# First filter layer over 64 rows, issued between the filter and the node sums; on ScalarE and VectorE the message ahead of the softplus

## The chip, the cores and the metric

The kernel runs on one core of a Trainium2 chip. Its time is the device time of one execution in microseconds (us). The five engines of the core run their own instruction streams side by side and meet at semaphores: TensorE (PE; its weight loads are listed as PEld), VectorE (DVE), ScalarE (ACT), GpSimd (POOL), and SyncE (SP), which here only issues transfers.

## The reference

One layer of a continuous-filter graph network over 6250 nodes and 200000 edges, sorted by `dst`:

```
h    = relu(layernorm(x))
y    = h @ W_in                                        # 6250 x 128
W_ij = (softplus(f_ij @ W_f1 + b_f1) - ln 2) @ W_f2 + b_f2   # per edge, f_ij has 20 values
m    = y[dst] * (W_ij * cutoff)                        # per edge
out  = segment_sum(m, src)                             # random scatter over the nodes
x    = x + (softplus(out @ W_o1 + b_o1) - ln 2) @ W_o2 + b_o2
```

## The kernel before

**Chunks and steps.** The edges are cut into 391 chunks of 512 (four tiles of 128). The main loop is written out as a sequence of steps k = -2, -1, 0, ...; in each step every engine does its part of several chunks, in an order fixed by the code (`hybrid_steps` calls each engine's `step`). Every engine executes its list strictly in that order and waits at semaphores.

**Two ways to sum.** Of every 25 chunks, 7 go "on PE" (108 in all): their messages are sorted into bins by matmuls with a 0/1 matrix (`bin_up`, L1289, seven tiles of four matmuls for each chunk), evacuated by ACT (`take_binned`, L729), and added to the nodes by further matmuls (`add_nodes`, L1308, twelve matmuls that alternate between rows 0 to 63 and 64 to 127 of the array). The other 283 chunks are "pool chunks": their rows with equal target are summed within a tile by `same_product` (L1275), evacuated by ACT (`take_sums`, L719 and L720), and added to memory by four indirect transfers that POOL issues (`scatter`, L598).

**The edge network of a chunk n.** `hidden_product` (L1258) is the first layer: two fp32 products of 256 edges each; the one takes rows 0 to 19 of `attrT` and `w_f1`, the other rows 64 to 83, so that they stand in two row groups of the array. Its results lie in PSUM banks 4 and 5. ACT does `softplus` in three dependent passes (L711 abs, L713 exp, L715 ln), DVE joins them with the product in `combine` (L1011), which raises `hidden_ready` (`s_h`). `filter_product` (L1266 for the bias, L1268 for the second layer) reads that. Beside it, PE fetches y[dst] by a product with a one-hot matrix (L1340, from `xwin`), ACT scales it by the cutoff (`xg`, L753), and DVE multiplies filter and xg to the message (L1099 for a pool chunk, L1096 for one on PE).

**Order in step k before.** PE: `same_product` of chunk k-2 (only if that is a pool chunk; its last quarter also waits for `hidden_ready` of chunk k, because it shares PSUM bank 5 with the first layer's result), an early `bin_up`, first layer of chunk k+1, one-hot product and filter of chunk k, one `add_nodes`, a late `bin_up`. ACT: `take_sums` of k-2, early `take_binned`, softplus of k+1, xg of k, late `take_binned`. DVE: one-hot of k+1 (L1036), node sums added (L1046), targets of k-2 (L1002, L1006), two node matrices (L1061), equality matrix of k (L995), places and payload of PE chunks (L1028, L1075, L1076, L1081), combine of k+1, message of k. There is one PSUM bank for binned tiles, so a `bin_up` waits until ACT has taken the one before (`binned_ready`).

Of the kernel before, what the change touches and what calls it, by code (L numbers as in the profile page):

```python
# [7 lines left out]
P = 128  # L8
T = 4
CE = P * T  # L10
# [12 lines left out]
def gnn_kernel(nc, x, src, src_cols, dst, dst_cols, attr_cols, cutoff_cols, W_in, W_f1, b_f1, W_f2, b_f2, W_o1, b_o1, W_o2, b_o2, out):  # L23
# [3 lines left out]
    N, F = x.shape  # L27
# [25 lines left out]
    with ctx:  # L53
        def sb(name, shape, dt=fp32):
            return ctx.enter_context(nc.sbuf_tensor(name, shape, dt))

        def sem(name):
            return ctx.enter_context(nc.semaphore(name))
# [11 lines left out]
        counting = sb("counting", [P, BINS * CAP], fp16)  # L70
        spare_row = sb("spare_row", [P, 1])
        w_in = sb("w_in", [P, F])
        w_f1 = sb("w_f1", [64 + RBF, F])
        w_f2 = sb("w_f2", [P, F])
        w_o1 = sb("w_o1", [P, F])
        w_o2 = sb("w_o2", [P, F])
# [82 lines left out]
        place_col = sb("place_col", [P, NPE, T])  # L159
        rank_max = sb("rank_max", [P, 1])  # L160

        attrT = sb("attrT", [64 + RBF, 4, CE // 2])
        dst_b = sb("dst_b", [P, 4, CE], bf16)
        src_b = sb("src_b", [P, 4, CE], i16)
        xwin = sb("xwin", [P, 4, F], bf16)
# [16 lines left out]
        s_cut = sem("cutoff_columns_loaded")  # L182
        s_iota = sem("iota_done")
        s_const = sem("constants_ready")
        s_zero = sem("zeros_ready")
        s_accz = sem("accumulators_cleared")
        s_centred = sem("centred_ready")
# [100 lines left out]
        def halves(columns):  # L288

            return columns.rearrange("p (r c) -> p r c", r=2)  # L290
# [12 lines left out]
        def exists(c):  # L303
            return 0 <= c < NCH
# [18 lines left out]
        def after(eng, semaphore, c):  # L323

            wait(eng, semaphore, c + 1)
# [69 lines left out]
        def hybrid_steps(step):  # L395

            for c in range(-2, LAST_STEP + 1):
                step(c)
# [37 lines left out]
        def _(sp):  # L436
# [58 lines left out]
            def reload_nodes():  # L495
                sp.dma_start(xs[:, :, :], x.rearrange("(p b) f -> p b f", b=NB)).then_inc(s_last, 16)

            for c in range(2):
                load_attr(c, c)
            sp.wait_ge(s_rows, 16 * 2 * G)  # L500
# [157 lines left out]
        def _(act):  # L658
# [4 lines left out]
            act.dma_start(bf1[:, :], b_f1.rearrange("(p o) -> p o", o=1)).then_inc(s_w, 16)  # L663
            for tile, a in ((bf2_row, b_f2), (bo2_row, b_o2)):
                act.dma_start(tile[:, :], a.rearrange("(o f) -> o f", o=1).to_broadcast([P, F])).then_inc(s_w, 16)
            for r in range(2):
                act.dma_start(w_f1[64 * r:64 * r + RBF, :], W_f1).then_inc(s_w, 16)

# [40 lines left out]
            def softplus(z, bias, a, steps, value):  # L709

                nc.scalar.activation(a, z, ACT.Abs, bias=bias).then_inc(steps[0], 1)  # L711
                act.wait_ge(steps[0], value)
                nc.scalar.activation(a, a, ACT.Exp, scale=-1.0).then_inc(steps[1], 1)  # L713
                act.wait_ge(steps[1], value)
                nc.scalar.activation(a, a, ACT.Ln, bias=1.0).then_inc(steps[2], 1)  # L715
# [15 lines left out]
            def hybrid_evacuations():  # L731
                def step(k):
                    n = k - 2
                    if pool_chunk(n):
                        wait(act, s_sp, pool_until(n))
                        after_scatters(act, pool_until(n - 4))
                        wait(act, s_moved, pool_until(n - 4))
                        take_sums(n % 4)
                    jobs = sorts_at.get(k, ())
                    for kk, h, i, late in jobs:  # L740
                        if not late:
                            take_binned(kk, h, i)
                    n = k + 1
                    if exists(n) and n > 0:
                        after(act, s_hp, n)
                        after(act, s_h, n - 2)
                        softplus(hidden_ps, bf1[:, 0:1], halves(hidden_exp[:, n % 2, :]), (s_size, s_exp, s_log), n + 1)
                    n = k
                    if exists(n):
                        after(act, s_xgp, n)  # L750
                        after(act, s_msg, n - 2)
                        for t in range(T):
                            last = nc.scalar.activation(xg[:, n % 2, t * F:(t + 1) * F], ps[3][:, t * F:(t + 1) * F], ACT.Copy,  # L753
                                                        scale=cut_col[:, bass.ds(n, 1), t])
                        last.then_inc(s_xg, 1)
                    for kk, h, i, late in jobs:
                        if late:
                            take_binned(kk, h, i)
                hybrid_steps(step)
# [47 lines left out]
        def _(dve):  # L807
# [8 lines left out]
            V = nc.vector  # L816
            V.memset(ones[:, :], 1.0)
            V.memset(ones_bf[:, :], 1.0)
            dve.wait_ge(s_iota, 3)
            V.tensor_scalar(ident[:, :], column_no[:, :], row_no[:, 0:1], None, ALU.is_equal)  # L820
            link(V.tensor_scalar(weight_bits[:, :], row_no[:, 0:1], -1.0, 127.0 + 63.0, ALU.mult, ALU.add))
# [187 lines left out]
            def combine(odd):  # L1009

                V.scalar_tensor_tensor(halves(hidden[:, odd, :]), hidden_ps, bf1_negative[:, 0:1], halves(hidden_exp[:, odd, :]),  # L1011
                                       ALU.max, ALU.add).then_inc(s_h, 1)

            def hybrid_work():
# [16 lines left out]
                def step(k):  # L1031
# [46 lines left out]
                    if on_pe(n):  # L1078
                        kk = pe_index[n]
                        wait(dve, s_mid, kk + 1)  # L1080
                        V.tensor_tensor(part_of(kk, 2), part_of(kk, 1), high_of(kk, 1), ALU.subtract).then_inc(s_pay, 1)  # L1081
                    n = k + 1
                    if exists(n) and n > 0:
                        after(dve, s_log, n)
                        after(dve, s_fp, n - 2)
                        combine(n % 2)
                    n = k
                    if exists(n):
                        after(dve, s_fp, n)
                        after(dve, s_xg, n)  # L1090
                        filtered = ps[2].rearrange("p (t f) -> p t f", t=T)
                        gate = xg[:, n % 2, :].rearrange("p (t f) -> p t f", t=T)
                        if on_pe(n):
                            kk = pe_index[n]
                            wait(dve, s_binps, (kk - 1) * JT)
                            V.tensor_tensor(payload[:, kk % 2, :, 0:F], filtered, gate, ALU.mult).then_inc(s_msg, 1)  # L1096
                        else:
                            wait(dve, s_sp, pool_until(n - 2))
                            V.tensor_tensor(message[:, n % 2, :, 0:F], filtered, gate, ALU.mult).then_inc(s_msg, 1)  # L1099
                hybrid_steps(step)  # L1100
                dve.wait_ge(s_accT, sums_until(NPE + SLOTS - 2, 1))

# [89 lines left out]
        def _(pe):  # L1192
# [61 lines left out]
            def hidden_product(slot):  # L1254

                for r in range(2):
                    rows = slice(64 * r, 64 * r + RBF)
                    ins = MM(hidden_ps[:, r, :], w_f1[rows, :], attrT[rows, slot, :], start=True, stop=True)  # L1258
                ins.then_inc(s_hp, 1)

# [52 lines left out]
            def hybrid_products():  # L1313
                def step(k):
                    n = k - 2
                    if pool_chunk(n):
                        wait(pe, s_same, pool_until(n))
                        after(pe, s_msg, n)
                        wait(pe, s_s, pool_until(n) - 1)
                        same_product(n % 2, range(T - 1))  # L1320
                        if exists(n + 2):
                            after(pe, s_h, n + 2)
                        same_product(n % 2, (T - 1,)).then_inc(s_sp, 1)
                    jobs = sorts_at.get(k, ())
                    for kk, h, i, late in jobs:
                        if not late:
                            bin_up(kk, h, i)
                    n = k + 1
                    if exists(n) and n > 0:
                        after_slot(pe, s_attr, n, 2)  # L1330
                        after(pe, s_h, n - 1)
                        wait(pe, s_last_sum, pool_until(n - 3))
                        hidden_product(n % 4)
                    n = k
                    if exists(n):
                        after(pe, s_oh, n)
                        after_slot(pe, s_xwin, n)
                        after(pe, s_xg, n - 1)
                        for t in range(T):
                            ins = MM(ps[3][:, t * F:(t + 1) * F], onehot[0:KW, n % 2, t * P:(t + 1) * P],  # L1340
                                     xwin[0:KW, n % 4, :], start=True, stop=True)
                        ins.then_inc(s_xgp, 1)
                        after(pe, s_h, n)
                        after(pe, s_msg, n - 1)
                        filter_product(n % 2)
                    for job in sums_at.get(k, ()):
                        add_nodes(*job)
                    for kk, h, i, late in jobs:
                        if late:
                            bin_up(kk, h, i)  # L1350
                hybrid_steps(step)
# [102 lines left out]
```

## Time and profile before

| | |
|---|---|
| median of 3 runs | 2415.03 us (2414.46 to 2416.0) |
| the profiled execution | 2413.26 us, of which the span is 2411.4 us |
| PE busy | 2207.1 us, 92% of the span |
| DVE busy | 1898.1 us, 79% |
| ACT busy | 1775.7 us, 74% |
| POOL busy | 1855.0 us, 77% |
| mean granted TensorE clock | 0.981 of full speed |

The page's section 1 gives busy shares, section 4 the chain of work that ended last (PE 71% of it), section 5 the costliest groups of instructions. A matmul's duration runs from its start to its modelled end and overlaps its neighbours; how much of PE's time a group takes is therefore read from the chain in order of time, where each piece begins at the end of the one before. Under 100 us at the start (layer norm, x W_in, sorting ranks) and some 90 us at the end (output layer) lie outside the main loop.

### The profile page before, as it was taken

The page shows a single profiled execution, that of the slowest core. Times are in us where ns is not written, and L with a number is a line of the kernel's source. Part 1 is how long each engine was busy: PE and PEld are TensorE (multiplying, and loading weights), DVE is VectorE, ACT ScalarE, POOL GpSimd, SP SyncE. Part 2 cuts the span into 40 slices and gives each one's busy share as a digit, 9 for nine tenths or more (in the row PEclk, how much of TensorE's full clock was granted, in tenths as well). Part 3 has the DMA queues.
Part 4 walks back from the last instruction along what each step waited for, and adds up shares of the span by engine and source line. Part 5 has one row for each costly group of instructions (what it writes and reads, how often), then busy time and mean ns, then how long its engine had stood idle before and what let it go on. Part 6 is the DMA issues. An engine that isn't in the chain of part 4 may idle for free.

```text
span 2411.4 us, 56737 instructions
## 1 busy us (share of the span) xinstructions
PE 2207.1 (92%) x16842; PEld 1401.0 (58%) x16842; DVE 1898.1 (79%) x3929; ACT 1775.7 (74%) x4145; POOL 1855.0 (77%) x1192
## 2 busy tenths in 40 slices
PE   1689999999999999999999999999999999999945
PEld 1566566566656656665665666566566656656623
DVE  8677877877787787878778777877887887788758
ACT  1578777777777777777777777777777777777713
POOL 2288888888887888788788888878887887888853
PEclk9899999999999999999999999999999999999968
DMA  9265556555555555555555555555555555555565
GB/s 354 100 99 91 88 88 90 87 88 88 90 87 87 90 89 88 88 90 87 87 89 87 89 89 90 86 87 91 86 89 88 89 86 88 90 87 88 81 162 180
DMA packets 351511, 239.84 MB, mean 99 GB/s; under 512 B 89459, under 2 KB 338497, under 8 KB 351071
## 3 DMA queue, kind: packets, MB, share of 16 engines
q0 software_dynamic: 164000, 77.47, 33.4%
q1 hardware_dynamic: 185987, 158.25, 24.1%
q8 instruction: 140, 2.29, 0.4%
q14 instruction: 172, 1.41, 0.2%
q10 hardware_dynamic: 1212, 0.42, 0.1%
HBM read 139.86 MB, written 96.12 MB: 98 GB/s over the span
## 4 chain that ended last, share of the span: by engine, by line
PE 71%; DMA 8%; issue 7%; DVE 5%; POOL 4%; ACT 4%; ACTq 0%; SPq 0%; POOLq 0%; DVEq 0%
PE ps L1289 20%; PE ps L1308 16%; PE ps L1268 11%; PE ps L1258 8%; PE ps L1275 8%; DMA acc<-region,target 7%; PE ps L1340 4%; POOL acc L598 4%; PE ps L1266 3%; ACT region L729 1%; ACT region L753 1%; ACT region L711 1%; ACT region L713 1%; DMA w_f<-in_L_gnn_W_f_dram 1%; DMA region<-in_x_dram 0%
## 5 line engine op out<-in xcount | busy, mean ns | idle before, releaser
L598 POOL DMA_INDIRECT acc<-region,target x1132 | 1797.1, 1588 | 424.5 <-issue 274.9
L1289 PE MATMUL ps<-region 128*128 128x386 bf16 x3024 | 650.0, 336 | 66.5 <-ACT region L729 46.6
L729 ACT ACTIVATE region<-ps 128x386 bf16<-128x386 f32 x756 | 372.3, 492 | 272.5 <-PE ps L1289 217.2
L1308 PE MATMUL ps<-region 64*128 64x448 bf16 x4536 | 497.8, 352 | 9.5 <-DVE region L1046 9.5
L1289 PEld LDWEIGHTS ps<-region 128*128 128x128 bf16 x3024 | 253.4, 97 | 367.6 <-issue 169.8
L1011 DVE SCALAR_TENSOR_TENSOR region<-ps,bf_negative,region 128x512 f32<-128x512 f32 x391 | 292.1, 747 | 210.3 <-ACT region L715 119.2
L753 ACT ACTIVATE region<-ps,cut_col 128x128 f32<-128x128 f32 x1564 | 439.0, 362 | 0.7 <-PE ps L1340 0.7
L1268 PEld LDWEIGHTS ps<-w_f,region 128*128 128x128 f32 x3128 | 414.7, 193 | 11.2
L1268 PE MATMUL ps<-w_f,region 128*128 128x128 f32 x3128 | 415.4, 276 | 0.0
L711 ACT ACTIVATE region<-ps,bf 128x512 f32<-128x512 f32 x391 | 268.6, 687 | 71.2 <-PE ps L1258 11.5
L1275 PEld LDWEIGHTS ps<-region 128*128 128x128 f32 x2264 | 294.0, 191 | 26.2 <-DVE region L1011 4.0
L1308 PEld LDWEIGHTS ps<-region 64*128 64x128 bf16 x4536 | 190.9, 94 | 197.2 <-issue 14.7
L1275 PE MATMUL ps<-region 128*128 128x129 f32 x2264 | 302.4, 275 | 2.4 <-DVE region L1011 1.3
L1061 DVE TENSOR_SCALAR region<-counting,region 128x448 bf16<-128x448 f16 x756 | 291.3, 425 | 9.0 <-PE ps L1308 8.3
L1258 PE MATMUL ps<-attrT,w_f 20*128 20x256 f32 x1564 | 276.1, 429 | 16.0 <-ACT region L719 7.3
L713 ACT ACTIVATE region<-region 128x512 f32<-128x512 f32 x391 | 246.4, 630 | 12.3
L715 ACT ACTIVATE region<-region 128x512 f32<-128x512 f32 x391 | 246.2, 630 | 12.4
L1099 DVE TENSOR_TENSOR region<-ps,region 128x512 f32<-128x512 f32 x283 | 194.8, 688 | 72.5 <-ACT region L753 38.8
L1002 DVE TENSOR_SCALAR moved<-region,weight_limit,spare_row 128x4 f32<-128x4 f32 x283 | 108.1, 382 | 126.5 <-ACT region L720 104.5
L1046 DVE TENSOR_TENSOR region<-region,ps 128x896 f32<-128x896 f32 x188 | 202.2, 1075 | 4.3 <-PE ps L1308 4.3
L1258 PEld LDWEIGHTS ps<-attrT,w_f 20*128 20x128 f32 x1564 | 118.3, 184 | 144.4 <-issue 144.4
L995 DVE TENSOR_TENSOR region<-src_b,src_col 128x512 f32<-128x512 int16 x283 | 195.6, 691 | 0.0
(128 smaller groups left out, 1700.0 us busy)
## 6 DMA issues: line engine op xcount, KB each, us to landing
dst_b<-dst_rows SPq DMA_DIRECT2D x391, 128.0 KB
src_b<-src_rows SPq DMA_DIRECT2D x283, 128.0 KB
acc<-region,target POOLq DMA_INDIRECT x1132
attrT<-in_edge_attr_dram SPq DMA_DIRECT2D x782, 20.0 KB
acc<-region SPq DMA_DIRECT2D x20, 640.0 KB, 17.4
xwin<-xw_parts SPq DMA_DIRECT2D x391, 31.5 KB
region<-acc SPq DMA_DIRECT2D x48, 256.0 KB, 4.5
xw_parts<-parts SPq DMA_DIRECT2D x12, 384.0 KB, 2.3
```

The costliest lines, as they stand in the source:

```text
L598: nc.gpsimd.indirect_dma_start(out=acc[a], out_offset=bass.IndirectOffsetOnAxis(ap=target[:, slot, t:t + 1], axis=0), in_=summed[:, slot, ...
L711: nc.scalar.activation(a, z, ACT.Abs, bias=bias).then_inc(steps[0], 1)
L713: nc.scalar.activation(a, a, ACT.Exp, scale=-1.0).then_inc(steps[1], 1)
L729: nc.scalar.activation(binned[:, h, j, :], binned_ps[:, 0:PC], ACT.Copy).then_inc(s_binned, 1)
L753: last = nc.scalar.activation(xg[:, n % 2, t * F:(t + 1) * F], ps[3][:, t * F:(t + 1) * F], ACT.Copy, scale=cut_col[:, bass.ds(n, 1), t])
L1011: V.scalar_tensor_tensor(halves(hidden[:, odd, :]), hidden_ps, bf1_negative[:, 0:1], halves(hidden_exp[:, odd, :]), ALU.max, ALU.add).then ...
L1061: V.tensor_scalar(in_node[:, sums_until(kk, i) % 2, slot, :], counting[:, 0:NL], binned[:, slot, j, 3 * F:3 * F + 1], binned[:, slot, j, 3 ...
L1258: ins = MM(hidden_ps[:, r, :], w_f1[rows, :], attrT[rows, slot, :], start=True, stop=True)
L1268: ins = MM(ps[2][:, t * F:(t + 1) * F], hidden[:, odd, t * P:(t + 1) * P], w_f2[:, :], start=False, stop=(t == T - 1), skip_group_check=True)
L1275: ins = MM(sums_ps[t], same[:, odd, t * P:(t + 1) * P], message[:, odd, t, :], start=True, stop=True)
L1289: ins = MM(binned_ps[:, 0:PC], place[:, h % 2, t, j * P:(j + 1) * P], payload_high[:, h % 2, t, :], start=(t == 0), stop=(t == T - 1))
L1308: ins = MM(ps[6 + r][:, 0:NL], binned[rows, slot, j, part * F:(part + 1) * F], in_node[rows, sums_until(kk, i) % 2, slot, :], start=(d == ...
```

## The change

The first layer now works on 64 rows in each half: `w_f1` and `attrT` are allocated with 128 rows, cleared by DVE at the very start, and only 20 rows of each half are loaded as before; the others stay zero. SP and ACT wait for the clearing before they load into them. In the main loop the first layer of chunk k+1 is issued after the filter of chunk k and directly ahead of `add_nodes`; on ACT xg of chunk k stands ahead of the softplus of k+1; on DVE the message of chunk k stands ahead of the combine of k+1. `general_*`, the path for other inputs, is not run here and keeps its order.

```diff
-        w_f1 = sb("w_f1", [64 + RBF, F])
+        w_f1 = sb("w_f1", [P, F])
-        attrT = sb("attrT", [64 + RBF, 4, CE // 2])
+        attrT = sb("attrT", [P, 4, CE // 2])
+            sp.wait_ge(s_blank, 2)
             for c in range(2):
                 load_attr(c, c)
+            act.wait_ge(s_blank, 1)
             for r in range(2):
                 act.dma_start(w_f1[64 * r:64 * r + RBF, :], W_f1).then_inc(s_w, 16)
...
             V.memset(ones_bf[:, :], 1.0)
+            V.memset(w_f1[:, :], 0.0).then_inc(s_blank, 1)
+            V.memset(attrT[:, :, :], 0.0).then_inc(s_blank, 1)
...
-                    rows = slice(64 * r, 64 * r + RBF)
+                    rows = slice(64 * r, 64 * r + 64)
                     ins = MM(hidden_ps[:, r, :], w_f1[rows, :], attrT[rows, slot, :], start=True, stop=True)
...
# PE, step k (ACT: softplus behind xg; DVE: combine behind the message, in the same manner)
-                    n = k + 1
-                    if exists(n) and n > 0:
-                        after_slot(pe, s_attr, n, 2)
-                        after(pe, s_h, n - 1)
-                        wait(pe, s_last_sum, pool_until(n - 3))
-                        hidden_product(n % 4)
                     n = k
                     if exists(n):
                         after(pe, s_oh, n)
...
                         filter_product(n % 2)
+                    n = k + 1
+                    if exists(n) and n > 0:
+                        after_slot(pe, s_attr, n, 2)
+                        after(pe, s_h, n - 1)
+                        wait(pe, s_last_sum, pool_until(n - 3))
+                        hidden_product(n % 4)
                     for job in sums_at.get(k, ()):
                         add_nodes(*job)
```

PE's list in the middle of the main loop, before: one step from `same_product` (L1275) to `add_nodes` (L1308). A bracket holds the semaphores an instruction waits for.

```order
L1275 MATMUL ps<-region 128x129 [waits sums_ready,message_ready,same_ready]
L1275 MATMUL ps<-region 128x129 x2
L1275 MATMUL ps<-region 128x129 [waits hidden_ready]
L1289 MATMUL ps<-region 128x386 [waits binned_ready]
L1289 MATMUL ps<-region 128x386 x3
L1258 MATMUL ps<-attrT,w_f 128x256 [waits last_sums_ready,hidden_ready,attr_loaded1]
L1258 MATMUL ps<-attrT,w_f 128x256
L1340 MATMUL ps<-xwin,onehot 128x128 [waits xg_ready,window_loaded0,onehot_ready]
L1340 MATMUL ps<-xwin,onehot 128x128 x3
L1266 MATMUL ps<-bf_parts,ones_bf 128x512 [waits message_ready,hidden_ready]
L1268 MATMUL ps<-w_f,region 128x128 x4
L1308 MATMUL ps<-region 128x448 [waits node_sums_added,in_node_ready]
```

The same step of the changed kernel, where the lines are 1280 for `same_product`, 1294 for `bin_up`, 1339 for the one-hot product, 1271 and 1273 for the filter, 1263 for the first layer and 1313 for `add_nodes`:

```order
L1280 MATMUL ps<-region 128x129 [waits sums_ready,message_ready,same_ready]
L1280 MATMUL ps<-region 128x129 x2
L1280 MATMUL ps<-region 128x129 [waits hidden_ready]
L1294 MATMUL ps<-region 128x386 [waits binned_ready]
L1294 MATMUL ps<-region 128x386 x3
L1339 MATMUL ps<-xwin,onehot 128x128 [waits xg_ready,window_loaded0,onehot_ready]
L1339 MATMUL ps<-xwin,onehot 128x128 x3
L1271 MATMUL ps<-bf_parts,ones_bf 128x512 [waits message_ready,hidden_ready]
L1273 MATMUL ps<-w_f,region 128x128 x4
L1263 MATMUL ps<-attrT,w_f 128x256 [waits last_sums_ready,hidden_ready,attr_loaded1]
L1263 MATMUL ps<-attrT,w_f 128x256
L1313 MATMUL ps<-region 128x448 [waits node_sums_added,in_node_ready]
```

The first layer moved behind five rows of one-hot product and filter; `hidden_ready`, which comes out of it, is still asked for by the last `same_product` of the next step and by its filter.

ACT's list in the same step, before: sums and binned tile taken, softplus, xg, binned tile.

```order
L719 ACTIVATE region<-ps 128x129 [waits scattered2,scattered3,scattered1,moved_ready,scattered0,sums_in_psum]
L720 ACTIVATE region<-ps 128x387
L729 ACTIVATE region<-ps 128x386 [waits node_sums_in_psum,binned_in_psum]
L711 ACTIVATE region<-ps,bf 128x512 [waits hidden_ready,hidden_in_psum]
L713 ACTIVATE region<-region 128x512 [waits hidden_size_ready]
L715 ACTIVATE region<-region 128x512 [waits hidden_exp_ready]
L753 ACTIVATE region<-ps,cut_col 128x128 [waits message_ready,xg_in_psum]
L753 ACTIVATE region<-ps,cut_col 128x128 x3
L729 ACTIVATE region<-ps 128x386 [waits node_sums_in_psum,binned_in_psum]
```

And of the changed kernel (722 and 723 are `take_sums`, 732 `take_binned`, 751 xg, 714 to 718 softplus):

```order
L722 ACTIVATE region<-ps 128x129 [waits scattered2,scattered3,scattered1,moved_ready,scattered0,sums_in_psum]
L723 ACTIVATE region<-ps 128x387
L732 ACTIVATE region<-ps 128x386 [waits node_sums_in_psum,binned_in_psum]
L751 ACTIVATE region<-ps,cut_col 128x128 [waits message_ready,xg_in_psum]
L751 ACTIVATE region<-ps,cut_col 128x128 x3
L714 ACTIVATE region<-ps,bf 128x512 [waits hidden_ready,hidden_in_psum]
L716 ACTIVATE region<-region 128x512 [waits hidden_size_ready]
L718 ACTIVATE region<-region 128x512 [waits hidden_exp_ready]
L732 ACTIVATE region<-ps 128x386 [waits node_sums_in_psum,binned_in_psum]
```

The three softplus passes moved behind xg and now stand directly ahead of the late `take_binned`.

## Rows read from the trace of the kernel before

**Rows 1.** Busy time by engine, 600 to 2200 us: PE, PEld, DVE, ACT, POOL, clock.
```profile
600.00:2200.00 1600.00, 1547.00 (x12045) 975.25 (x12042) 1274.21 (x2723) 1254.01 (x2955) 1297.99 (x819) 1.00 0.58 88
```
**Rows 2.** The chain in order of time: start us, length us, what.
```profile
1206.30 0.58 issue
1206.88 0.87 PE ps L1289 x4
1207.75 0.63 PE ps L1258 x4
1208.38 0.33 PE ps L1340 x4
1208.71 0.22 PE ps L1266
1208.92 0.89 PE ps L1268 x8
1209.82 1.24 PE ps L1308 x12
1211.06 0.80 PE ps L1289 x4
1211.86 0.89 PE ps L1275 x8
1212.75 0.69 PE ps L1289 x4
```
**Rows 3.** Timeline of ACT: start us, us, instruction [idle before it <- releaser].
```profile
1206.33 0.49 ACT L729 ACTIVATE region<-ps 128x386 bf16<-128x386 f32 x1 [0.42 <-PE ps L1289]
...
1208.42 0.69 ACT L711 ACTIVATE region<-ps,bf 128x512 f32<-128x512 f32 x1
1209.14 0.63 ACT L713 ACTIVATE region<-region 128x512 f32<-128x512 f32 x1
1209.80 0.63 ACT L715 ACTIVATE region<-region 128x512 f32<-128x512 f32 x1
1210.34 1.12 ACT L753 ACTIVATE region<-ps,cut_col 128x128 f32<-128x128 f32 x4
...
1212.78 0.28 ACT L719 ACTIVATE region<-ps 128x129 f32<-128x129 f32 x1 [0.40 <-DMA acc<-region,target]
1212.96 0.49 ACT L720 ACTIVATE region<-ps 128x387 f32<-128x387 f32 x1
```
**Rows 4.** Timeline of DVE over one of its steps.
```profile
1206.00 0.69 DVE L1099 TENSOR_TENSOR region<-ps,region 128x512 f32<-128x512 f32 x1 [0.30 <-issue]
1206.61 0.34 DVE L1036 TENSOR_SCALAR onehot<-dst_b,row_in_window 126x512 bf16<-126x512 bf16 x1
1206.87 1.08 DVE L1046 TENSOR_TENSOR region<-region,ps 128x896 f32<-128x896 f32 x1
1207.86 0.84 DVE L1061 TENSOR_SCALAR region<-counting,region 128x448 bf16<-128x448 f16 x2
1208.63 0.67 DVE L995 TENSOR_TENSOR region<-src_b,src_col 128x512 f32<-128x512 int16 x1
1209.23 0.44 DVE L1028 TENSOR_SCALAR region<-counting,place_col 128x896 bf16<-128x896 f16 x1
1209.59 0.68 DVE L1081 TENSOR_TENSOR region<-region 128x512 f32<-128x512 f32 x1
1210.47 0.75 DVE L1011 SCALAR_TENSOR_TENSOR region<-ps,bf_negative,region 128x512 f32<-128x512 f32 x1 [0.20 <-ACT region L715]
```
**Rows 5.** Groups of instructions: POOL's scatters, busy us, mean ns, idle us before.
```profile
L598 POOL DMA_INDIRECT acc<-region,target x1132 | 1797.1, 1588 | 424.5 <-issue 274.9 <-DVE target L1006 81.6 <-DMA acc<-region,target 68.0
```
**Rows 6.** Timeline of the first 20 us, POOL and DVE.
```profile
1.11 1.16 POOL L572 MEMSET region<- 128x1280 f32 x1
...
3.13 0.29 DVE L820 TENSOR_SCALAR ident<-column_no,row_no 128x128 f32<-128x128 f32 x1 [1.99 <-POOL counting L573]
...
18.02 0.15 DVE L838 TENSOR_SCALAR bo_negative<-bo 128x1 f32<-128x1 f32 x1 [2.58 <-DMA w_f<-in_L_gnn_W_f_dram]
```

More of the change, by code:

```diff
@@ L184, in gnn_kernel @@
         s_const = sem("constants_ready")
+        s_blank = sem("rows_past_the_rbf_cleared")
         s_zero = sem("zeros_ready")
@@ L742, in step @@
                             take_binned(kk, h, i)
-                    n = k + 1
-                    if exists(n) and n > 0:
-                        after(act, s_hp, n)
-                        after(act, s_h, n - 2)
-                        softplus(hidden_ps, bf1[:, 0:1], halves(hidden_exp[:, n % 2, :]), (s_size, s_exp, s_log), n + 1)
                     n = k
@@ L755, in step @@
                         last.then_inc(s_xg, 1)
+                    n = k + 1
+                    if exists(n) and n > 0:
+                        after(act, s_hp, n)
+                        after(act, s_h, n - 2)
+                        softplus(hidden_ps, bf1[:, 0:1], halves(hidden_exp[:, n % 2, :]), (s_size, s_exp, s_log), n + 1)
                     for kk, h, i, late in jobs:
@@ L1081, in step @@
                         V.tensor_tensor(part_of(kk, 2), part_of(kk, 1), high_of(kk, 1), ALU.subtract).then_inc(s_pay, 1)
[L1082 to L1086, printed above, removed]
                     n = k
@@ L1099, in step @@
                             V.tensor_tensor(message[:, n % 2, :, 0:F], filtered, gate, ALU.mult).then_inc(s_msg, 1)
+                    n = k + 1
+                    if exists(n) and n > 0:
+                        after(dve, s_log, n)
+                        after(dve, s_fp, n - 2)
+                        combine(n % 2)
                 hybrid_steps(step)
@@ L1327, in step @@
                             bin_up(kk, h, i)
-                    n = k + 1
-                    if exists(n) and n > 0:
-                        after_slot(pe, s_attr, n, 2)
-                        after(pe, s_h, n - 1)
-                        wait(pe, s_last_sum, pool_until(n - 3))
-                        hidden_product(n % 4)
                     n = k
@@ L1345, in step @@
                         filter_product(n % 2)
+                    n = k + 1
+                    if exists(n) and n > 0:
+                        after_slot(pe, s_attr, n, 2)
+                        after(pe, s_h, n - 1)
+                        wait(pe, s_last_sum, pool_until(n - 3))
+                        hidden_product(n % 4)
                     for job in sums_at.get(k, ()):
```

## The prediction

> **What bounds the kernel now.** I read the engines' shares first, then the chain in order of time, then the timelines of ACT and DVE around one step. In the 1600 us in the middle PE is busy for 1547, at clock 1.00; DVE, ACT and POOL for 1274 to 1298 [rows 1]. The chain in order of time shows two kinds of step [rows 2]. From 1206.30 to 1211.86 is one without `same_product`: it begins with 0.58 us of waiting, and lasts 0.58+0.87+0.63+0.33+0.22+0.89+1.24+0.80 = 5.56 us. With `same_product` (L1275) the step has no gap: 0.89+0.69+0.63+0.33+0.22+0.89+1.24+0.80 = 5.69 us, one PE piece behind the other. So PE itself is the bound in the second kind. In the first kind it waits for one thing: the late binned tile ends on PE at 1206.30, ACT takes it from 1206.33 for 0.49 [rows 3], and the next `bin_up` starts at 1206.88, 0.06 after ACT's end. POOL issued 1132 scatters, four for each pool chunk [rows 5], so 283 steps are of the kind with `same_product` and 108 of the 391 of the other. POOL is near a bound too: (1.588 + 0.30) x 4 = 7.55 us for each pool chunk, and with 18 pool chunks in 25 that is 5.44 us a step; the 0.30 is its `issue` idle, 274.9 us over most of 874 scatters' gaps [rows 5].
>
> **What PE saves.** A group of matmuls costs its columns plus something at a change of row groups. Four `bin_up` matmuls take 0.69 behind the full-height L1275 and 0.80 behind the 64-row L1308: 0.11 for that change. The one-hot product takes 0.33 for 4x128 bf16 columns, L1266 takes 0.22 for 512: again 0.11 too much, behind the 20-row first layer [rows 2]. L1308 takes 1.24 for six pairs of 448 columns, at 0.22 for 512 that is 1.16 (a pair runs side by side): up to 0.1 for its change. Before, a step went full, 20 rows, full, 64 rows, full: four changes. After, it goes full, 64 rows (first layer and node sums), full: two. The two that go away are worth 0.11 + 0.12 = 0.23 us a step. The Trainium skill (TensorEngine Tiling, Key Properties) says that changing the tiling mode, not just the tile, drains TensorE; the excesses just read agree, and by that rule alone the change is a gain, which I carry as a rival below.
>
> **What 64 rows instead of 20 cost.** No row shows a 64-row fp32 product of 256 columns. Lower end: nothing, as the same four matmuls stream the same columns. Upper end: the two halves no longer run side by side. L1268 takes 0.89 for eight fp32 matmuls of 128 columns, 0.11 each, so 256 columns are 0.22 and four in a row 0.88, against the 0.63 of now with its change of rows included (two pairs, 0.44, and 0.19): +0.44. Twelve 64-row matmuls in 1.24 do run side by side in pairs [rows 2], which is the nearer row, so I take 0. The Trainium skill (TensorE: Matmul & The Clock Gate, LDWEIGHTS) says that loading weights costs by columns and not by rows, so that the taller operand is free; were time to go by rows, 64/20 of the 0.44 would be 1.4 us, and the step +0.97. The trace of before cannot show which, as no group changes its height alone.
>
> **What the new order costs: the path through `hidden_ready`.** Before, PE had filter, node sums, late bin and same_product between a first layer and the next need of its softplus. After, one-hot product and filter are ahead of the first layer. Measure from the end of the first layer's last matmul, H:
> 1. ACT starts 0.04 later (1208.38 to 1208.42), its three passes end 2.01 later (1209.80+0.63-1208.42) [rows 2, 3]. ACT is free by then: xg, four passes in 1.12, starts once the one-hot product is done, and that is 0.22+0.89+0.63 = 1.74 before H.
> 2. DVE starts 0.04 after that (1210.43 to 1210.47) and takes 0.75 [rows 4]; PE sees it about 0.06 later, as in the hand-over above. Together H + 2.90.
> 3. PE meanwhile: node sums 1.12 (without change of rows), late bin 0.80, three quarters of same_product 0.67, so it stands at H + 2.59, and the last quarter must wait. It would have been through at H + 2.81; it now starts at 2.90 and is through about 0.40 later (one fp32 pitch of 0.11 and an end that lags by a matmul's length; I take 0.3 to 0.5), at H + 3.30. So 0.49 of waiting.
> 4. Then early bin 0.69, one-hot 0.22, L1266 0.22, filter 0.89, first layer 0.63 = 2.65, and the loop closes: 5.95 us, against 5.69. That is +0.26 in each of 283 steps (+0.16 to +0.36).
>
> The four matmuls behind the waiting one, and everything of PE after them, stand still for these 0.49; nobody else can use it, since ACT and DVE are the ones waited for.
>
> **The steps without same_product.** There the early bin waits for ACT's take of the late tile, as before. The late take now stands behind softplus: it can start 1.96 after H (where L753 started, 1210.34 - 1208.38 [rows 2, 3]); the late tile itself is on PSUM at H + 1.92. So 1.96+0.49+0.06 = H + 2.51 for PE, then 0.87+0.22+0.22+0.89+0.63 = 2.83: 5.34 us against 5.56, -0.22 in each of 108 steps. `hidden_ready` at H + 2.90 is needed by the filter only at H + 3.6, covered. If the take came 0.2 later, the gain would be gone; if sooner, it is 0.25 at most.
>
> **DVE and POOL.** On DVE the message of k now comes ahead of combine k+1, and DVE stands idle between them. All the rest waits behind combine: from L1036 to the end of L1081 is 3.66 [rows 4], the two target instructions are about 0.4, the message 0.69. From combine's end at H + 2.84 that is H + 7.6, and the next combine is wanted at H + 5.95 + 2.09 = H + 8.0: 0.4 to spare in the fullest step. `take_sums` ends at 3.30+0.04+0.66 = H + 4.0 (0.28 and 0.49, overlapping [rows 3]), as DVE has done L1036 and L1046 (H + 4.1). The node sums of the next step need L1046 by H + 5.95: covered. POOL needs 5.44 a step and gets 5.78, so its idle grows; nothing there is late. SP's loads hang on first layers and one-hot products three steps back and keep their lead.
>
> **The start.** The two memsets fall into DVE's idle 1.99 us ahead of L820; 1280 columns took 1.16 on POOL, attrT has 1024. The weights' DMA, issued later than that, is what DVE waits for at 18.02 [rows 6]. Cost between 0 and 1 us; I take 0.
>
> **Sum.** 283 x 0.26 - 108 x 0.22 = 73.6 - 23.8 = +50 us. On the profiled execution's 2413.3 (span 2411.4 and 1.9 around it; 1.8 below the median of the runs) that is 2463, and 2465 as a median. The balance point is near: at +0.08 in place of +0.26 a step the two kinds cancel.
>
> **Rivals.**
> A. *PE sets the pace and the drains pay* (faster). If `hidden_ready` were there by H + 2.6, a step would be 5.46, the other kind 5.33, together 5.42, and POOL's 5.44 would bind: from 5.65 now that is -0.21 x 391 = -82, so 2333. For it: four changes become two, and PE is the bound now. Against it: three passes and a combine take 2.84 in rows that waited for nothing else. It decides in the last quarter of same_product; the chain would have to be 0.3 shorter than measured. The tiling page's rule points here.
> B. *The two kinds cancel* (no change, 2415): needs 0.18 less in item 3, for instance a last quarter of 0.2 instead of 0.40.
> C. *DVE comes late to combine* (slower still). With 0.4 to spare in the fullest step, one more wait (node matrices on a tile not yet taken, a target on a late scatter) of 0.8 would push 0.4 into 100 to 283 steps: +40 to +110 on top, about 2520. Against: most steps lack L1046 or the payload and have over 1 us.
> D. *The halves serialize at 64 rows*: +0.44 x 391 = +172, 2637.
>
> **Numbers.** Forecast 0.72, A 0.08, B 0.06, C 0.11, D 0.03. The forecast's own range is 2435 to 2493 (+-0.10 x 283). From B and C I widen to 2428 to 2512. About 0.2% (5 us) is what a measurement tells from no change. Faster: A and a share of the forecast's low end, 0.09; within 0.2%: 0.05; slower: 0.86.
>
> **What would show it.** In the chain after: an idle piece of about 0.5 ahead of the last two matmuls of L1280, released by DVE L1016; the one-hot product at 0.22; first layer and node sums 0.63 + about 1.12; steps of 5.95 and 5.34. DVE idle ahead of L1016 near 1.3 to 2 us, ended by ACT L718. PE's busy sum lower, POOL's idle higher, clock still 1.00, as it was with the 0.58 gaps. The forecast is wrong if steps with same_product are under 5.75, if L1016 starts later than 0.1 after L718, or if L1263 takes over 0.8.

## The result, and the profile after

The changed kernel takes 2503.29 us (median of 4, 2496.76 to 2504.72) against 2415.34; the ratio is 1.0364, 95% interval 1.0347 to 1.0381: slower. That is inside the stated range of 2428 to 2512 but 10 above the forecast's own range of 2435 to 2493; the +50 of the sum became +88. The profiled execution took 2502.56 us, its span 2500.7, 89.3 more than before.

The chain in order of time over one step of each kind (start us, length us, what), which answers to [rows 2]. Its `issue` pieces of 0.02 to 0.06 between the others are left out:

```profile
1206.20 0.49 PE ps L1280 x2
1206.69 0.69 PE ps L1294 x4
1207.39 0.23 PE ps L1339 x4
1207.67 1.05 PE ps L1273 x8
1208.72 0.66 PE ps L1263 x4
1209.40 0.70 ACT region L714
1210.12 0.64 ACT region L716
1210.78 0.64 ACT region L718
1211.45 0.76 DVE region L1016
1212.25 0.49 PE ps L1280 x2
1212.74 0.69 PE ps L1294 x4
1213.43 0.23 PE ps L1339 x4
1213.66 0.22 PE ps L1271
1213.88 0.89 PE ps L1273 x8
1214.77 0.63 PE ps L1263 x4
1215.40 1.14 PE ps L1313 x12
1216.54 0.81 PE ps L1294 x4
1217.37 0.50 ACT region L732
1217.92 0.86 PE ps L1294 x4
```

Before, the chain in the middle of the loop had nothing but PE between two gaps; now it leaves PE in every step. With same_product it runs first layer, three softplus passes on ACT, combine on DVE, the last two matmuls of same_product, early bin, one-hot, filter, first layer: from 1206.20 to 1212.25, 6.05 us. The node sums (L1313) are not in it: they stand beside softplus. In a step without same_product (from 1215.40 on) it runs over the late tile's take by ACT, as before. The one-hot product takes 0.23 now and not 0.33, the node sums 1.14 and not 1.24: the two saved changes of row groups are there, and the second is not on the path of a step with same_product.

The groups of section 5 that matter, after (busy us, mean ns | idle us before, what ended it); the second answers to [rows 4], the fourth to [rows 5]:

```profile
L1280 PE MATMUL ps<-region 128*128 128x129 f32 x2264 | 374.8, 288 | 102.1 <-DVE region L1016 102.1
L1016 DVE SCALAR_TENSOR_TENSOR region<-ps,bf_negative,region 128x512 f32<-128x512 f32 x391 | 293.5, 751 | 433.4 <-ACT region L718 433.4
L1263 PE MATMUL ps<-attrT,w_f 64*128 64x256 f32 x1564 | 277.4, 432 | 0.0
L600 POOL DMA_INDIRECT acc<-region,target x1132 | 1833.1, 1619 | 476.3 <-issue 264.1
```

PE idles 102 us ahead of the last two matmuls of same_product, and DVE 433 us ahead of combine. PE's idle is 0.30 us in such a step and understates the loss, since it is counted from the modelled end of the matmul before; a section below gives the loss as 0.57. The first layer's mean is 432 ns where it was 429 at 20 rows. Between 600 and 2200 us the engines read (PE, PEld, DVE, ACT, POOL busy, granted clock), against [rows 1]:

```profile
600.00:2200.00 1600.00, 1482.53 (x11513) 1006.67 (x11651) 1190.51 (x2633) 1190.75 (x2860) 1282.29 (x792) 1.00 0.57 85
```

PE, DVE, ACT and POOL execute fewer instructions in the same time (11513 matmuls for 12045), at the same clock: a wait, not slower work. Only the weight loads (PEld) have a higher busy sum.

**Where the 89 us are.** The first layer's 391 starts give the steps. From the 17th on, 374 steps took 0.196 us more each on average (+73). The first sixteen took 104.3 us (97.10 to 201.4) where they had taken 87.0 (97.27 to 184.3): +17. The end gave 1 back. PE's timeline at the start of the loop shows why the first steps lose more:

```profile
108.58 0.58 PE L1339 MATMUL ps<-xwin,onehot 126*128 126x128 bf16 x4 [10.78 <-DMA xwin<-xw_parts]
...
111.23 1.23 PE L1263 MATMUL ps<-attrT,w_f 64*128 64x256 f32 x4
112.39 0.61 PE L1339 MATMUL ps<-xwin,onehot 126*128 126x128 bf16 x4
115.36 0.39 PE L1271 MATMUL ps<-bf_parts,ones_bf 128*128 128x512 bf16 x1 [2.36 <-DVE region L1016]
```

The first window of y arrives near 108.5 us in both kernels. Before, the first layer of chunk 1 ran ahead of that wait; now it queues behind it. And until node sums and bins set in, nothing covers softplus: several steps that took 5.02 before take 5.33 or 6.05. The clock is no part of it: from 95 to 210 us it is 0.87 in both traces.

### The profile page after: what moved, and what is told of

The parts are those of the page before. It is cut to its first block, busy times and chain, and to the rows that moved or that the text cites. A ratio compares the mean times of both kernels' runs of the same rounds, so it can differ in the third digit from the quotient of the medians.

```text
span 2500.7 us, 56544 instructions
## 1 busy us (share of the span) xinstructions
PE 2187.3 (87%) x16647; PEld 1488.1 (60%) x16842; DVE 1841.4 (74%) x3931; ACT 1745.4 (70%) x4145; POOL 1894.8 (76%) x1192
## 4 chain that ended last, share of the span: by engine, by line
PE 55%; ACT 24%; DVE 13%; issue 4%; DMA 2%; POOL 1%; ACTq 0%; SPq 0%; DVEq 0%; POOLq 0%
PE ps L1273 15%; PE ps L1294 14%; PE ps L1263 10%; DVE region L1016 8%; ACT region L714 8%; ACT region L716 7%; ACT region L718 7%; PE ps L1280 5%; PE ps L1313 5%; PE ps L1339 3%; ACT region L732 2%; PE ps L1271 2%; POOL acc L600 1%; DMA acc<-region,target 1%; DMA w_f<-in_L_gnn_W_f_dram 0%
## 5 line engine op out<-in xcount | busy, mean ns | idle before, releaser
L600 POOL DMA_INDIRECT acc<-region,target x1132 | 1833.1, 1619 | 476.3 <-issue 264.1
L1313 PE MATMUL ps<-region 64*128 64x448 bf16 x4536 | 494.6, 350 | 9.3 <-DVE region L1051 9.3
L1280 PE MATMUL ps<-region 128*128 128x129 f32 x2264 | 374.8, 288 | 102.1 <-DVE region L1016 102.1
L751 ACT ACTIVATE region<-ps,cut_col 128x128 f32<-128x128 f32 x1564 | 445.0, 375 | 4.7 <-PE ps L1339 4.7
L1280 PEld LDWEIGHTS ps<-region 128*128 128x128 f32 x2264 | 314.2, 190 | 179.5 <-DVE region L1016 156.1
L1313 PEld LDWEIGHTS ps<-region 64*128 64x128 bf16 x4536 | 228.4, 94 | 198.0 <-issue 14.0
L1066 DVE TENSOR_SCALAR region<-counting,region 128x448 bf16<-128x448 f16 x756 | 278.8, 410 | 8.6 <-PE ps L1313 8.2
L1263 PE MATMUL ps<-attrT,w_f 64*128 64x256 f32 x1564 | 277.4, 432 | 0.0
L722 ACT ACTIVATE region<-ps 128x129 f32<-128x129 f32 x283 | 78.7, 278 | 275.1 <-PE ps L1280 209.7
L1007 DVE TENSOR_SCALAR moved<-region,weight_limit,spare_row 128x4 f32<-128x4 f32 x283 | 95.8, 339 | 151.6 <-ACT region L723 144.1
```

Of the source, the lines that this page charges most:

```text
L600: nc.gpsimd.indirect_dma_start(out=acc[a], out_offset=bass.IndirectOffsetOnAxis(ap=target[:, slot, t:t + 1], axis=0), in_=summed[:, slot, ...
L1280: ins = MM(sums_ps[t], same[:, odd, t * P:(t + 1) * P], message[:, odd, t, :], start=True, stop=True)
L1313: ins = MM(ps[6 + r][:, 0:NL], binned[rows, slot, j, part * F:(part + 1) * F], in_node[rows, sums_until(kk, i) % 2, slot, :], start=(d == ...
```

## The experiments

All ran against the kernel before; a ratio carries its 95% interval. The theory is the one of the prediction: the path first layer, softplus, combine, last quarter of same_product. The rivals were the height of 64 rows, the move on PE as such, and DVE's order.

**Height alone.** The kernel before, with the clearing and 64 rows, order as before.

```diff
-                    rows = slice(64 * r, 64 * r + RBF)
+                    rows = slice(64 * r, 64 * r + 64)
```

> The kernel before with the clearing and with 64 rows in the first layer, order as before. Theory (the loss is the path from the first layer through softplus and combine to the last quarter of same_product, the height is free): within 5 us of before, 2410 to 2420; L1258's successor still pays its change of row groups, first-layer piece 0.63 to 0.66. Rival (the taller first layer costs by itself, 0.03 to 0.4 us in each of 391 steps, as PE has no slack in this order): +12 to +170 us.

2411.97 us, 0.9988 (0.9978 to 0.9997). The first layer's piece in the chain is 0.63, as with 20 rows. The one-hot product still takes 0.33 and the node sums 1.24. The height costs nothing; that also settles the serial halves (rival D).

**Order alone.** The changed kernel with `rows = slice(64 * r, 64 * r + RBF)`.

> The changed kernel with 20 rows in the first layer, new order kept. Theory (path through hidden_ready; the saved change of row groups stands beside a wait): a pool step unchanged at 6.05, since 0.11 to 0.2 more on PE between first layer and node sums only eats the 0.5 of waiting; a step without same_product 5.34 to 5.46 as the late tile comes 0.1 later; so 2498 to 2518. Rival (the height is what costs): back towards 2415 to 2465.

2516.34 us, 1.0421 (1.0403 to 1.0438). Its chain in order of time, from the node sums on:

```profile
1204.76 1.24 PE ps L1313 x12
1206.00 0.80 PE ps L1294 x4
1206.80 0.67 PE ps L1280 x6
1207.47 0.19 issue
1207.66 0.49 PE ps L1280 x2
```

The node sums cost 1.24 again. Steps with same_product are still 6.04 to 6.05; those without went from 5.35 to 5.45. So the saved change is worth 0.10 in 103 steps, 10.5 of the 12.7 us between the two spans, and nothing where PE waits anyhow; the first sixteen steps give the other 2.4.

**Only PE's move.** The changed kernel with ACT (softplus, then xg) and DVE (combine, then message) in the order of before.

```diff
# ACT, step k
+                    n = k + 1
+                    if exists(n) and n > 0:
...
+                        softplus(hidden_ps, bf1[:, 0:1], halves(hidden_exp[:, n % 2, :]), (s_size, s_exp, s_log), n + 1)
                     n = k
                     if exists(n):
                         after(act, s_xgp, n)
```

> The changed kernel with ACT's and DVE's order as before (softplus ahead of xg, combine ahead of the message); only PE's move and the 64 rows are left. Theory: after the first layer's end H the late tile is taken behind softplus and xg, at H+3.6; so every step, of either kind, becomes 3.6+0.87+0.23+0.22+0.89+0.66 = 6.4 to 6.5: 2700 to 2760. Rival (the cost is the move on PE, whatever ACT and DVE do): 2495 to 2515.

2716.52 us, 1.1249 (1.1230 to 1.1268). ACT's timeline:

```profile
1200.87 0.69 ACT L714 ACTIVATE region<-ps,bf 128x512 f32<-128x512 f32 x1 [1.49 <-PE ps L1263]
...
1202.78 1.13 ACT L756 ACTIVATE region<-ps,cut_col 128x128 f32<-128x128 f32 x4
1203.78 0.51 ACT L732 ACTIVATE region<-ps 128x386 bf16<-128x386 f32 x1
```

ACT waits 1.49 for the first layer with xg, whose input is long there, queued behind softplus; the late tile is taken at 1203.78, about H + 2.9, and nearly every step is 6.36. The moves on ACT and DVE are what kept the change at +88; ACT's alone is worth 196 us, by the next run, which differs from this one in ACT's order only.

**DVE's order as before.** PE and ACT as changed.

> The changed kernel with DVE's order as before (combine of k+1 ahead of the message of k), PE and ACT as changed. Theory: combine stays at H+2.07 to 2.84, the message comes at H+2.8 to 3.5, and PE asks for it at H+4.5; so the time stays at 2503, 2495 to 2510: DVE's part of the change bears nothing. Rival (DVE's order matters as ACT's does): over 2530.

2520.39 us, 1.0432 (1.0416 to 1.0448). Neither forecast: 17 above the changed kernel where I had said the same. Steps with same_product stay at 6.05, those without are 5.49 and not 5.35. The message is now made behind combine and ends about H + 3.4. PE asks for it with the weight load of the bias product (L1271), which in the changed kernel starts with the last one-hot matmul, 0.17 sooner than here:

```profile
1205.13 0.68 DVE L1104 TENSOR_TENSOR region<-ps,region 128x512 f32<-128x512 f32 x1
1205.93 0.10 PEld L1271 LDWEIGHTS ps<-bf_parts,ones_bf 128*128 128x128 bf16 x1
```

In 119 steps from the 17th on (those without same_product or without an early bin) that load is late, and each time it starts 0.115 or 0.116 us after the message's end; in the changed kernel it is late in none. 119 x 0.14 is 17 us; with 3 more in the first sixteen steps that is the 19 between the two spans. I had counted PE's request as H + 3.6, to the end of the one-hot product's columns. PE's own start shows the same wait uncovered, with L1104 the message:

```profile
115.42 0.59 PE L1271 MATMUL ps<-bf_parts,ones_bf 128*128 128x512 bf16 x1 [3.14 <-DVE region L1104]
```

**The path shortened.** The third pass of softplus (ln) left out in the main loop, so the output is not the reference's; in the changed kernel, and in the kernel before.

```diff
-                nc.scalar.activation(a, a, ACT.Exp, scale=-1.0).then_inc(steps[1], 1)
-                act.wait_ge(steps[1], value)
-                nc.scalar.activation(a, a, ACT.Ln, bias=1.0).then_inc(steps[2], 1)
+                nc.scalar.activation(a, a, ACT.Exp, scale=-1.0).then_inc(steps[2], 1)
```

> The changed kernel without the third pass of softplus (the ln) in the main loop, so its output is not the reference's. Theory: hidden_ready comes 0.66 sooner, at H+2.21, before PE asks at H+2.61: pool step 5.49, the other kind 5.34; POOL near its bound; 2350 to 2380. Rival (the wait belongs to something else than the length of this path): 2480 to 2503.

> The kernel before, with the same pass left out. Theory: in this order softplus stands beside filter, node sums and bins, PE is the bound: 2405 to 2417. Rival (the shorter path helps wherever it is, so that the changed order is not what exposes it): 2415 less up to 0.6 x 283 = 2245.

2354.33 us, 0.9757 (0.9742 to 0.9773), for the one; 2404.82, 0.9957 (0.9942 to 0.9973), for the other. The same 0.66 us of work is worth 149 us in the new order and 10 in the old one (6 of these in nine steps from the 17th on that took 5.02 and now take 4.36, 2.5 in the first sixteen). The pass also frees ACT of as much work in both orders, so ACT's load alone does not explain the 149. Without the pass the changed kernel's steps are mostly 5.48 and 5.35; from its chain in order of time:

```profile
1208.11 0.89 PE ps L1278 x8
```

L1278 is same_product: eight matmuls in 0.89, unbroken.

**Last quarter later.** The changed kernel, complete, with same_product's last quarter moved behind the one-hot product; on ACT the early tile ahead of the sums.

```diff
-                        if exists(n + 2):
-                            after(pe, s_h, n + 2)
-                        same_product(n % 2, (T - 1,)).then_inc(s_sp, 1)
...
                         ins.then_inc(s_xgp, 1)
+                    n = k - 2
+                    if pool_chunk(n):
+                        if exists(n + 2):
+                            after(pe, s_h, n + 2)
+                        same_product(n % 2, (T - 1,)).then_inc(s_sp, 1)
```

> The changed kernel with the last quarter of same_product moved behind the one-hot product, directly ahead of the filter, and on ACT the early binned tile ahead of the sums. Nothing is left out. Theory: hidden_ready is now asked for at H+3.5 and is there at H+2.87, so the wait of 0.5 goes and PE's pace is 5.46 to 5.5 in pool steps; POOL's 5.44 to 5.5 is then next: 2345 to 2375, faster than before. Rival (DVE's late combine and what queues behind it hold the step): stays at 2480 to 2505.

2390.36 us, 0.9900 (0.9883 to 0.9917): the wait for `hidden_ready` is gone and the kernel is 1.0% faster than before, but 15 short of the forecast. The chain says where:

```profile
1213.04 0.67 PE ps L1280 x6
1213.71 0.78 PE ps L1294 x4
1214.48 0.23 PE ps L1336 x4
1214.71 0.28 PE ps L1280 x2
```

The step is mostly 5.62: the early bin takes 0.78 for 0.69 and the last quarter 0.28 for 0.22, which I had not counted. The 0.09 of the early bin is another wait. With two fp32 matmuls fewer ahead of it, its first weight load asks for the PSUM bank sooner, and ACT has not finished taking the late tile:

```profile
1213.08 0.49 ACT L732 ACTIVATE region<-ps 128x386 bf16<-128x386 f32 x1
1213.62 0.46 PEld L1294 LDWEIGHTS ps<-region 128*128 128x128 bf16 x4
```

The load starts 0.05 after that take ends, and so it does, as the median, in the 247 such steps from 210 us on. The 0.06 goes to the first fp32 matmul behind the one-hot product.

**One-hot product first.** To keep same_product whole: one-hot product between late bin and same_product.

> The changed kernel with the one-hot product issued first in PE's step, between the late bin_up and an undivided same_product. Nothing is left out. Theory: from H, PE is at the last quarter at 1.14+0.80+0.23+0.67 = H+2.84, where hidden_ready comes at H+2.87: the wait goes without dividing same_product. Pool step 1.14+0.80+0.23+0.89+0.69+0.22+0.89+0.63 = 5.49; the other kind 2.52+0.87+0.22+0.89+0.63 = 5.13, as the one-hot product stands in the wait for the late tile; mean 5.39, below POOL's (1.60+0.30) x 4 x 0.72 = 5.47. So POOL becomes the bound, 2355 to 2385, less than the 2390 of the divided version. Rival (dividing cost nothing and something else set 5.62 there): 2385 to 2395.

2413.19 us, 0.9991 (0.9982 to 1.0000): a miss by 28 us or more, and the most telling one.

```profile
1207.89 0.72 PE ps L1280 x6
1208.62 0.01 issue
1208.63 0.49 PE ps L1280 x2
```

Short steps are 5.12 as forecast, the others 5.82 and not 5.49. The chain leaves an idle piece of 0.01 only, as I had reckoned 0.03, yet the last quarter takes 0.49, as behind the long wait. I read that as a price of refilling, about 0.27, that comes on top of any wait, and built the next forecast on it. The weight loads show otherwise:

```profile
1207.68 0.75 PEld L1280 LDWEIGHTS ps<-region 128*128 128x128 f32 x6
1208.63 0.30 PEld L1280 LDWEIGHTS ps<-region 128*128 128x128 f32 x2 [0.20 <-DVE region L1016]
```

It is the load that waits for `hidden_ready`. In an unbroken row (the run without ln) the seventh load starts 0.11 ahead of its matmul, at 1208.51, and the sixth matmul ends at 1208.78: the load is due 0.27 before the end at which I had PE "arrive". Here it started 0.28 late, and the group is done 0.28 late. The forecast had the right path and asked for its result 0.27 too late. The other 0.05 of the 0.33 are six matmuls that take 0.72 behind the one-hot product and not 0.67.

**One-hot product and bias first.** The bias product of the filter needs no `hidden_ready`; it goes ahead too, so that the last quarter comes 0.22 later. On ACT xg stands first.

```diff
# PE
                         ins.then_inc(s_xgp, 1)
+                        after(pe, s_msg, n - 1)
+                        filter_bias()
...
                         after(pe, s_h, n)
-                        after(pe, s_msg, n - 1)
                         filter_product(n % 2)
```

> The changed kernel with PE's one-hot product and the bias part of the filter issued first in the step (late bin_up, one-hot, bias, undivided same_product, early bin_up, filter, first layer, node sums), and on ACT xg first (xg, sums, early tile, softplus, late tile). Nothing is left out. Theory: a wait on TensorE costs its length plus about 0.27 of refilling (as seen when the last quarter takes 0.49 behind a wait and 0.22 without one), so the wait must vanish altogether. PE gets to the last quarter at 1.14+0.80+0.23+0.22+0.67 = H+3.06, behind hidden_ready at H+2.90. Pool step 5.49; the other kind 2.52+0.87+0.89+0.63 = 4.91; mean 5.33, so POOL's about 5.45 binds: 2350 to 2370. Rival (the divided version's 2390 is the best this order gives, since something else than the wait sets PE's pace): 2385 to 2415.

2363.97 us, 0.9786 (0.9772 to 0.9800): complete, 2.1% faster than before and 5.6% faster than the changed kernel. Steps are mostly 4.91 and 5.60 (5.49 was forecast); the waiting load is still 0.12 late in a step with same_product, which is the difference. POOL's scatters, against [rows 5]:

```profile
L600 POOL DMA_INDIRECT acc<-region,target x1132 | 1807.6, 1597 | 365.8 <-issue 253.0 <-DMA acc<-region,target 81.1 <-DVE target L1011 28.6
```

Of the 366 us of idle 253 are the 0.30 between two scatters. That is the bound named in the prediction, (1.597 + 0.30) x 4 x 0.72 = 5.46 us a step; the 374 steps from the 17th on average 5.47.

**The same with 20 rows.**

> The same kernel with 20 rows in the first layer. Theory: where PE does not wait, a change of row groups between first layer and node sums costs 0.11 a step; pool step 5.60, the other kind up to 5.02; mean 5.44, at POOL's bound, so 2355 to 2385, that is 5 to 20 us above the version with 64 rows. Rival (64 rows bring nothing in any order, as in the kernel before): the same time as the version with 64 rows, within 3 us.

2370.88 us, 0.9821 (0.9805 to 0.9836): 7 us above the version with 64 rows, but not for the reason forecast. Short steps are mostly 5.01 for 4.91, the others 5.60 in both, and the 374 steps from the 17th on take 2046.3 us together against 2045.6: POOL sets their mean. The whole difference of the two spans, 6.8 us, lies in the first sixteen steps (101.6 against 94.0 us), where the granted clock differs. The window from 98 to 200 us, with 20 rows and with 64 (the 0.77 and 0.92 are the clock):

```profile
98.00:200.00 102.00, 79.74 (x480) 55.80 (x480) 60.42 (x130) 64.98 (x157) 63.48 (x41) 0.77 0.50 88
98.00:200.00 102.00, 75.24 (x536) 52.79 (x536) 67.26 (x144) 71.05 (x171) 67.10 (x44) 0.92 0.54 98
```

The mean clock is 0.973 to 0.975 in all five runs with 20 rows and 0.977 to 0.983 in those with 64. Whether the rows bring that about is not shown.

**What the wait costs, over all orders.** PE's timeline has the eight matmuls of same_product as one row (start us, length us): without ln, one-hot and bias first with 20 rows, the same with 64 rows, one-hot first.

```profile
1207.95 1.05 PE L1278 MATMUL ps<-region 128*128 128x129 f32 x8
1205.19 1.07 PE L1283 MATMUL ps<-region 128*128 128x129 f32 x8
1212.97 1.17 PE L1283 MATMUL ps<-region 128*128 128x129 f32 x8
1207.73 1.39 PE L1280 MATMUL ps<-region 128*128 128x129 f32 x8
```

The next table sets the lateness of the seventh load (median of some 270 chunks, against a start 0.11 behind the sixth load) beside the step with same_product. PE's own pace is 5.48 as measured without ln, plus 0.10 where 20 rows bring the change of row groups back, plus 0.05 where same_product follows the one-hot product.

| order | load late | PE's own pace | sum | step measured |
|---|---|---|---|---|
| changed kernel | 0.57 | 5.48 | 6.05 | 6.05 |
| changed, 20 rows | 0.46 | 5.58 | 6.04 | 6.04 |
| one-hot first | 0.29 | 5.53 | 5.82 | 5.82 |
| one-hot and bias first | 0.12 | 5.48 | 5.60 | 5.60 |
| the same, 20 rows | 0.02 | 5.58 | 5.60 | 5.60 |

A wait costs its own length and nothing more, if it is measured where the load is due; a load 0.02 late costs 0.02. The 0.10 of the height is lost in every one of these steps, because the load is that much later when PE comes that much sooner.

## Why the prediction came out as it did

- **Mechanism and place: right.** An idle piece released by combine ahead of the last two matmuls of same_product was forecast and is there; leaving out 0.66 us of the path gave 149 us back.
- **Item 1 and 2, the path up to `hidden_ready`: right.** From the first layer's start to the start of the last quarter 0.63 + 2.90 = 3.53 was forecast; the chain has 0.66 + 2.87. (Its first layer is 0.66 where the chain goes on to ACT and 0.63 where it goes on to PE.)
- **Item 3, the last quarter: mis-sized.** I took 0.40 (0.3 to 0.5); it is 0.49 in every step with same_product, 0.22 for two matmuls in a row and 0.27 by which a matmul's end lags behind the start of the next load. With 0.01 more for the one-hot product the step is 6.05 and not 5.95, that is +0.36 in place of +0.26. The trace of before had the row. In its first steps same_product waits for combine too:

```profile
138.16 0.76 DVE region L1011
...
138.96 0.49 PE ps L1275 x2
```

- **Steps without same_product: right.** 5.34 forecast, 5.35 measured.
- **Saved changes of row groups: nearly right,** 0.10 each for 0.11 and 0.12. The order with 20 rows isolates the one ahead of the node sums, and it is hidden as forecast. The one ahead of the one-hot product came with its new predecessor, so no run shows it by itself.
- **Height: right** at 0. The Trainium skill (TensorE: Matmul & The Clock Gate, LDWEIGHTS) says that a weight load's time goes by columns and not by rows. The trace agrees: the first layer's loads take 184 ns on average with 20 rows and 186 with 64.
- **The start: missed.** I costed the memsets (nothing, rightly) but not the first steps of the loop, where the move puts a first layer behind the first window's arrival and softplus has no cover: +17 us.
- **The sum.** From the 17th step on, by what PE's list holds in a step:

| steps | before | after | total |
|---|---|---|---|
| 246 with same_product, early bin and all node sums | 5.69 | 6.04 or 6.05 | +88 |
| 103 without same_product | 5.55 or 5.56 | 5.34 or 5.35 | -21 |
| 15 with same_product, without an early bin | 5.53 | 5.35 or 5.36 | -3 |
| 9 with same_product, without all of the node sums | 5.02 or 5.12 | 6.04 | +9 |

With one step more (+0.3), the first sixteen (+17) and the end (-1) that is the 89. The forecast knew the first two kinds only.
- **The range.** It held the result because it had been widened for rival C, which did not occur. The two terms that were missing, 0.10 in the last quarter and the start, were not in it; that 2503 lies inside is in part luck.
- **Rival A** (PE sets the pace) is near what the kernel becomes once the wait is gone or nearly so: 2354 without ln and 2364 with one-hot product and bias first, where 2333 was reckoned. **Rival C** (DVE late to combine) did not occur: DVE idles 433 us there.

## What to carry to other kernels

Before a producer is moved back in an in-order stream, trace its result through the other engines to its next user in PE's own list, and count the cover that is left. Here 4.15 us of PE's work stood between the first layer and the last quarter of same_product; the move took 1.44 of it away and the saved change of row groups 0.10, and the 2.61 left do not cover a path of 2.9. Placing independent work between the two (one-hot product and bias) turned a loss of 88 us into a gain of 50. Count to the start of the weight load that carries the wait and not to the end of the matmul before it: in these fp32 rows that is 0.27 us sooner, and a forecast that counted to the end missed by 28 us.

## What the runs showed of the hardware that was not expected

- The wait of a matmul for a semaphore stands at its weight load. In an unbroken row of fp32 matmuls of 129 columns the loads start 0.11 us apart, each 0.11 ahead of its matmul and 0.27 ahead of the modelled end of the matmul before. A result that comes later than that delays PE by just as much: 0.57, 0.46, 0.29, 0.12 and 0.02 us in five orders.
- In the chain two such matmuls therefore take 0.22 in a row and 0.49 behind a semaphore, however short the idle piece ahead of them. The 0.27 between is no cost of its own.
- The first fp32 matmul behind the one-hot product's four bf16 matmuls of 128 columns costs 0.05 to 0.06 more (0.28 for two, 0.72 for six, against 0.22 and 0.67).
- Twelve 64-row matmuls of 448 columns take 1.14 behind a 64-row group and 1.24 behind one of 20 rows or of full height.
